# Products with block-diagonal adjacencies as 64 by 64 pieces in the four quarters of TensorE's array, with another order of steps

## The reference

```python
# layer 0: two hypergraph convolutions, G = D^-1 H B^-1 H^T from H = (adj != 0), with layer norm between
h = layer_norm(relu(G @ (x @ W1.T) + b1), gamma, beta)      # 512 -> 1024
y = G @ (h @ W2.T) + b2 + x                                  # 1024 -> 512
# layer 1: pairwise attention
A = exp(leaky(tanh((s_i + s_j) / 8) * 8)) * adj;  A = A / rowsum(A) * rowsum(adj);  y = A @ x @ w
# layer 2: three graph convolutions, relu after the first two
x = relu(adj @ (x @ W1) + b1); x = relu(adj @ (x @ W2) + b2); y = adj @ (x @ W3) + b3
# layer 3: attention of 8 heads over the 64 nodes, plus 0.33 * adj + 0.33 * exp(-adj), then an output projection
```

## Time and profile before

| | |
|---|---|
| median of 3 runs | 3037.49 us |
| lowest, highest | 3035.02, 3038.24 us |
| span of the profiled execution, first to last instruction | 3035.8 us |
| PE busy | 2912.6 us, 96% |
| PE weight loads busy | 2497.7 us, 82% |
| DVE busy | 2008.2 us, 66% |
| ACT, POOL busy | 922.4, 908.4 us, 30% each |
| one round of stage one | 76.50 us |
| one round of stage two | 106.0 to 106.1 us |

### The profile page before, as it was taken

The page is one execution under the profiler, slowest core; times in us unless marked ns, Lnnn a source line. Parts: engine busy times, 40 slices in busy tenths (PEclk is TensorE's granted clock), DMA queues, the critical chain, the costliest instruction groups (busy, mean ns, idle before and its releaser), DMA issues.

```text
span 3035.8 us, 50423 instructions
## 1 busy us (share of the span) xinstructions
PE 2912.6 (96%) x17944; PEld 2497.7 (82%) x17944; DVE 2008.2 (66%) x5274; ACT 922.4 (30%) x2525; POOL 908.4 (30%) x1619
## 2 busy tenths in 40 slices
PE   6999999999999999869999999999999999999998
PEld 4888888888888888658888888888888888888887
DVE  5888888888888888645455546545554654555465
ACT  2222222222222222133333324333332433333243
POOL 1222222222222222241342243134224313422431
PEclk9999999999999999979999999999999999999999
DMA  5000000000000000020010001001000100100000
GB/s 166 25 29 29 29 29 29 29 29 29 29 29 29 27 28 26 25 74 19 13 30 29 7 25 30 18 13 30 28 6 26 30 18 13 30 28 6 27 28 15
DMA packets 84785, 88.30 MB, mean 29 GB/s; under 512 B 46096, under 2 KB 46096, under 8 KB 84752
## 3 DMA queue, kind: packets, MB, share of 16 engines
q1 hardware_dynamic: 84752, 87.88, 9.5%
HBM read 54.28 MB, written 33.55 MB: 29 GB/s over the span
## 4 chain that ended last, share of the span: by engine, by line
PE 51%; DVE 3%; ACT 2%; DMA 1%; issue 0%; POOL 0%; DVEq 0%; POOLq 0%; SPq 0%
PE qsB L1070 30%; PE qsA L1070 16%; ACT E L941 2%; PE qsA L1136 2%; DVE E L1037 1%; PE qsA L1151 1%; PE qsA L1112 1%; PE qsA L1144 1%; PE qsB L1144 1%; DVE E L1024 1%; DMA X<-x 0%; DVE lo L970 0%; DMA QK<-in_L_Wqkv 0%; PE qsB L1086 0%; ACT hi L954 0%
## 5 line engine op out<-in xcount | busy, mean ns | idle before, releaser
L841 POOL TENSOR_SCALAR sm<-sm 128x1 f32<-128x1 f32 x128 | 28.5, 222 | 1064.9 <-DVE sm L987 1064.7
L982 DVE TENSOR_TENSOR T2l<-qsA,T2h 128x512 fp32r<-128x512 f32 x320 | 214.5, 683 | 198.0 <-ACT T2h L920 155.3
L219 POOL TENSOR_SCALAR sm<-sm 128x1 f32<-128x1 f32 x192 | 70.5, 367 | 835.8 <-DVE sm L430 666.8
L1070 PE MATMUL qsB<-hi,T2h 128*128 128x512 f32 x768 | 316.7, 412 | 1.4 <-DVE T2l L982 1.4
L1070 PE MATMUL qsB<-lo,T2h 128*128 128x512 f32 x768 | 304.1, 396 | 0.0
L1070 PE MATMUL qsB<-hi,T2l 128*128 128x512 f32 x768 | 303.9, 396 | 0.0
L941 ACT ACTIVATE E<-E,sm 128x128 f32<-128x128 f32 x512 | 198.2, 389 | 51.0 <-DVE sm L1028 51.0
L924 ACT ACTIVATE H<-H 128x512 f32<-128x512 f32 x128 | 81.0, 633 | 415.5 <-DVE H L1002 415.5
L541 PE MATMUL psA<-W2h,Th 128*128 128x512 f32 x512 | 205.1, 401 | 0.0
L541 PE MATMUL psA<-W2h,Tl 128*128 128x512 f32 x512 | 202.2, 395 | 0.0
L541 PE MATMUL psA<-W2l,Th 128*128 128x512 f32 x512 | 202.2, 395 | 0.0
(11 more groups left out here) (215 smaller groups left out, 8358.5 us busy)
## 6 DMA issues: line engine op xcount, KB each, us to landing
X<-in_x SPq DMA_DIRECT2D x64, 256.0 KB, 2.6
x<-R SPq DMA_DIRECT2D x64, 256.0 KB, 2.0
X<-x SPq DMA_DIRECT2D x64, 256.0 KB, 2.8
out<-Z SPq DMA_DIRECT2D x64, 256.0 KB, 2.9
A<-in_adj SPq DMA_DIRECT2D x256, 16.0 KB, 1.9
E<-in_L_W1T SPq DMA_DIRECT2D x4, 512.0 KB, 7.9
E<-in_L_W SPq DMA_DIRECT2D x4, 512.0 KB, 5.4
E<-in_L_Wqkv SPq DMA_DIRECT2D x2, 768.0 KB, 5.5
```

The costliest lines, as they stand in the source:

```text
L219: pool.tensor_scalar(col(c, VE), col(c, MV + 1), EPS, None, ALU.add).then_inc(ve, 1)
L982: return dve.tensor_tensor(lo, ps, hi.bitcast(F32), ALU.subtract)
L1070: mm = pe.matmul(out, lhsT, rhs, start=i == 0, stop=i == len(terms) - 1)
```

## The change

The 128 by 128 product becomes four products of 64 by 64 pieces: for each half of the features (q, which is also the half of the array's columns and of the output's rows) and each graph (g, the half of the array's rows), only the graph's own block is streamed, 64 columns. The zeros are left out. Each graph has its own bank: graph 0 writes psA, graph 1 psB, at 64 columns for each 128 features. The two banks of a chain are now one tensor `ps[c]`, and the evictions read both banks in one instruction.

```diff
-            def mix(out, rows, M):
-                for j in range(KD):
-                    f = slice(j * P, (j + 1) * P)
-                    mm = products(out[:, f], [(rows[:, f], M)])
+            def mix(c, rows, M, n):
+                for k in range(n):
+                    for q in (slice(0, C), slice(C, P)):
+                        for g, bank in ((slice(0, C), psA[c]), (slice(C, P), psB[c])):
+                            mm = pe.matmul(bank[q, k * C:(k + 1) * C], rows[g, k * P + q.start:k * P + q.stop], M[g, g],
+                                           start=True, stop=True)
                 return mm
+            def alone(sem, value):
+                pe.wait_ge(consts_ok, 4)
+                pe.wait_ge(sem, value)
             def tx(c, n, loaded):
-                pe.wait_ge(gt_sb, n[c])
+                alone(gt_sb, n[c])
                 pe.wait_ge(x_in[c], loaded)
                 pe.wait_ge(z2, n[c])
-                mix(psA[c][:, :], X[:, c, :], GT[:, c, :]).then_inc(tx_ps, 1)
+                pe.wait_ge(g1_sb, n[c])
+                mix(c, X[:, c, :], GT[:, c, :], KD).then_inc(tx_ps, 1)
             def t2(c, n):
-                pe.wait_ge(rc_ok, n[c])
+                alone(rc_ok, n[c])
                 pe.wait_ge(g2_ok, n[c])
-                mix(psA[c][:, :], R[:, c, 0:D], GT[:, c, :]).then_inc(t2_psA, 1)
-                mix(psB[c][:, :], R[:, c, D:DH], GT[:, c, :]).then_inc(t2_psB, 1)
+                mix(c, R[:, c, :], GT[:, c, :], KH).then_inc(t2_psA, 1)
...
-                products(psB[c][:, P:P + 1], [(Fp[:, c, :], ones[:, 0:1])])
-                mix(psA[c][:, :], R[:, c, D:DH], Fp[:, c, :]).then_inc(t3_ps, 1)
+                products(psB[c][:, 3 * P:3 * P + 1], [(Fp[:, c, :], ones[:, 0:1])])
+                mix(c, R[:, c, D:DH], Fp[:, c, :], KD).then_inc(t3_ps, 1)
...
             def txe(c, n):
                 act.wait_ge(tx_ps, n[c])
-                act.copy(Th[:, c, 0:D], psA[c][:, :]).then_inc(t1h, 1)
+                act.copy(by_graph(Th, c), halves(c)).then_inc(t1h, 1)
```

More of the change, by code:

```diff
@@ L90, in col, with halves, by_graph @@
             return sm[:, c, k:k + n]
-        psA = [ctx.enter_context(nc.psum_tensor(f"psA{c}", [P, D], F32)) for c in range(CH)]
-        psB = [ctx.enter_context(nc.psum_tensor(f"psB{c}", [P, D], F32)) for c in range(CH)]
+        ps = [ctx.enter_context(nc.psum_tensor(f"ps{c}", [P, 2, D], F32)) for c in range(CH)]
+        psA, psB = [ps[c][:, 0, :] for c in range(CH)], [ps[c][:, 1, :] for c in range(CH)]
+        def halves(c):
+            return ps[c][:, :, 0:KD * C].rearrange("p g (k j) -> p k g j", k=KD)
+        def by_graph(W, c, n=KD):
+            return W[:, c, 0:n * P].rearrange("p (k g j) -> p k g j", k=n, g=2)
         consts_ok, ident0 = sem("consts_ok"), sem("ident0")
@@ L288, in t2e @@
                 act.wait_ge(t2_psA, n[c])
-                act.copy(Th[:, c, 0:D], psA[c][:, :]).then_inc(t2hA, 1)
-                act.wait_ge(t2_psB, n[c])
-                act.copy(Th[:, c, D:DH], psB[c][:, :]).then_inc(t2hB, 1)
+                act.copy(by_graph(Th, c, KH)[:, :, 0, :], psA[c].rearrange("p (k j) -> p k j", k=KH)).then_inc(t2hA, 1)
+                act.copy(by_graph(Th, c, KH)[:, :, 1, :], psB[c].rearrange("p (k j) -> p k j", k=KH)).then_inc(t2hB, 1)
             def s8(c, n):
@@ L306, in t3e @@
                 act.wait_ge(t3_ps, n[c])
-                act.copy(Th[:, c, 0:D], psA[c][:, :]).then_inc(t3h, 1)
+                act.copy(by_graph(Th, c), halves(c)).then_inc(t3h, 1)
             def w(i):
@@ L395, in txe @@
                 dve.wait_ge(t1h, n[c])
-                dve.tensor_tensor(Tl[:, c, 0:D], psA[c][:, :], Th[:, c, 0:D].bitcast(F32), ALU.subtract).then_inc(t1_sb, 1)
+                dve.tensor_tensor(by_graph(Tl, c), halves(c), by_graph(Th, c).bitcast(F32), ALU.subtract).then_inc(t1_sb, 1)
             def relu(c, n, stored):
@@ L453, in t3e @@
             def t3e(c, n):
[L454 to L455 removed]
+                dve.wait_ge(t3h, n[c])
+                dve.reciprocal(col(c, RI), psB[c][:, 3 * P:3 * P + 1]).then_inc(ri_ok, 1)
                 dve.wait_ge(ri_ok, n[c])
                 dve.tensor_tensor(col(c, CI), col(c, RI), ATc[:, c, P:P + 1], ALU.mult)
[L458 to L459 removed]
+                dve.tensor_tensor(by_graph(Tl, c), halves(c), by_graph(Th, c).bitcast(F32), ALU.subtract).then_inc(t3_sb, 1)
             def z_second(c, n, after):
@@ L721, in col, with halves, by_graph @@
             return sm[:, c, k:k + n]
-        psA = [ctx.enter_context(nc.psum_tensor(f"qsA{c}", [P, D], F32)) for c in range(CH)]
-        psB = [ctx.enter_context(nc.psum_tensor(f"qsB{c}", [P, D], F32)) for c in range(CH)]
+        ps = [ctx.enter_context(nc.psum_tensor(f"qs{c}", [P, 2, D], F32)) for c in range(CH)]
+        psA, psB = [ps[c][:, 0, :] for c in range(CH)], [ps[c][:, 1, :] for c in range(CH)]
+        def halves(c):
+            return ps[c][:, :, 0:KD * C].rearrange("p g (k j) -> p k g j", k=KD)
+        def by_graph(W, c):
+            return W[:, :, c * P:(c + 1) * P].rearrange("p k (g j) -> p k g j", g=2)
         consts_ok, ident0, blocks0, bias_in, split_hi, split_lo = map(sem, (
@@ L919, in steps @@
                         act.wait_ge(t_ps[i], n[c])
-                        act.copy(T(Th, c), by_chunk(psA[c])).then_inc(th[i], 1)
+                        act.copy(by_graph(Th, c), halves(c)).then_inc(th[i], 1)
                     if step in ("g0", "g1"):
@@ L997, in steps @@
                         dve.wait_ge(th[i], n[c])
-                        rest(T(Tl, c), by_chunk(psA[c]), T(Th, c)).then_inc(t_sb[i], 1)
+                        rest(by_graph(Tl, c), halves(c), by_graph(Th, c)).then_inc(t_sb[i], 1)
                     if step in ("g0", "g1"):
@@ L1065, in _, with alone @@
             pe.wait_ge(consts_ok, 5)
+            def alone(sem, value):
+                pe.wait_ge(consts_ok, 5)
+                pe.wait_ge(sem, value)
             def products(out, terms):
@@ L1096, in steps @@
                         if i == 0:
-                            pe.wait_ge(at_sb, n[c])
+                            alone(at_sb, n[c])
                             pe.wait_ge(x_in[c], x_loaded[ahead])
                         else:
-                            pe.wait_ge(g_sb[i - 1], n[c])
+                            alone(g_sb[i - 1], n[c])
+                        rows = (H if i else X)[:, c, :]
                         for k in range(KD):
-                            f = slice(k * P, (k + 1) * P)
-                            mm = products(psA[c][:, f], [((H if i else X)[:, c, f], AT[:, c, :])])
+                            for q in (slice(0, C), slice(C, P)):
+                                for g, half in ((slice(0, C), psA[c]), (slice(C, P), psB[c])):
+                                    mm = pe.matmul(half[q, k * C:(k + 1) * C], rows[g, k * P + q.start:k * P + q.stop], AT[g, c, g],
+                                                   start=True, stop=True)
                         mm.then_inc(t_ps[i], 1)
```

10 lines of the change are left out of this document (6 added, 4 removed), and 24 rows, old and new, of the table ORDER.

## The result

The changed kernel takes 3065.3 us, the median of 4 runs (3062.38 to 3065.84). The kernel before, run beside it, takes 3037.2 us, also 4 runs. The ratio is 1.0094, with a 95% interval of 1.008 to 1.0108: slower by 0.9%. I had forecast 3012 us and a small gain. The time lies in the range that I gave, but on the wrong side of no change.

The account below looks back on a forecast made before the run. TensorE was taken to set the end: its work falls 5.45 and 3.8 us a round in stages one and two, added waits return 4.0 and 3.7, leaving 25 us saved over 16 rounds: 3012 us, range 2940 to 3090.

Parts of the forecast that it names:

- two at a time: Rival: the array's four quarters work only two at once, 0.90 us a run, 3085 us in all; chance 0.14.
- issue alone: Rival: issuing products at some 0.06 us each sets a run's time, 1.0 us, 3130 us in all; chance 0.08.
- feeding binds: Rival: handing products to TensorE limits a run to 0.64 us, 3033 us in all; chance 0.11.
- (a): Stage one: deg.0+ behind [tx.3 t2.1 t2.2] waits 1.6 us for inc.0+ from VectorE.
- (b): Stage one, after y2.2: deg.2+ waits 1.25 us for z1.2 and inc.2+, then y3.0 0.35 us for t3e.0.
- (c): Stage one: y3.1 after [t3.1 tx.0+] waits 0.8 us for z1.3 and t3e.1.
- (d): Stage one: tx.1+ and tx.2+ wait 0.2 and 0.15 us for z2; y3.3 waits 0.3, y2.3 0.1.
- (e): Stage two: g2.1 after [t2.1 t1.3 t2.2] waits 1.35 us, plus 0.1 for t2.2's relu.
- (f): Stage two, [t1.1 t2.0 t1.2 t0.3]: t1.2 waits 0.4 us for its relu, g2.0 1.1 for t2.0's eviction.
- (h): Stage two: av.2 waits 1.1 us for VectorE's copy of ta.2; g0.0+, behind z4.1 and av.3, waits 0.65.
- (i): Stage two: ta.2's wait for the softmax of s.2 falls from 1.97 to 0.45 us, with 0.4 before av.1.
- Nothing else is large: Both stages: beyond TensorE's work and the waits, evictions from two banks, added waits and DMAs taken to add about nothing.

Follow-up runs that it names:

- q_rot: The changed kernel with y1.2 and y2.0 moved from the end of stage one's TensorE loop to its head, same sequence; 3022.84 us, ratio 0.9957.
- w_neworder: Whole 128 by 128 products as in the kernel before, in both new orders; 3025.33 us, 0.9965 of the kernel before.
- part: Kernel before with quarters for t2 in stage one; stage two in new order, quarters for four steps only; 40 added instructions; 3020.3 us, ratio 0.9946.
- half: `q_rot` with stage two's evictions of t0, t1 and t2 covering half the columns in its rounds; 2995.85 us, 0.9866 of the kernel before.
- pad158: The changed kernel with 158 more instructions on TensorE's queue ahead of stage one's loop; 3043.2 us.
- q_oldorder: Quarter products with both stages' orders as in the kernel before; 3053.89 us, 1.0059 of the kernel before.

## Why the prediction was wrong

**What a run costs in quarters: right.** In `q_rot` the products of two t2 steps, four runs, stand as one group:

```profile
450.71 2.09 PE L577 MATMUL ps<-GT,R 64*64 64x64 f32 x128
```

Less some 0.24 us that the last takes to land, that is 1.85/4 = 0.46 us a run. All four quarters work at once, and no handover binds. The rivals "two at a time" (0.90) and "issue alone" (1.0) are out, and so is "feeding binds" (0.64). Two neighbouring runs of a chain each start 0.47 to 0.51 us apart (410.40 to 410.91 for t3.1 and tx.0+), so 0.45 was a little low.

**The evictions at no cost: right.** VectorE's rest out of both banks takes 685 ns in stage two and 678 to 684 in stage one, against 683 and 667 to 690 before (the earlier trace rows shows two of these).

**The waits: right in size.** Stage one, in `q_rot`: (a) 1.59 for 1.6, (b) 1.21 for 1.25 but nothing for the 0.35 before y3.0, (c) 0.84 for 0.8, (d) 0.31 twice for 0.2 and 0.15; TensorE idle for 75.50 - 71.05 = 4.45 of the 4.75 forecast. Stage two: (e) 1.01 for 1.35, (f) 0.34 and 0.71 for 0.4 and 1.1, (g) 0.50 for 0.5, (h) 0.86 and 1.24 for 1.1 and 0.65, (i) 0.52 and 0.32 for 0.45 and 0.4; idle (1396.20 - 1322.91)/13 = 5.6 of 6.0. `w_neworder` shows that the same order hardly waits when the products are whole, and `part` and `half` that the waits are for the evictions.

**The step that failed: "Nothing else is large".** I asked of each part what it adds to VectorE, to the banks and to the waits, and of the instructions only what it costs to hand them over. Their number nearly doubled in stage one's loop, and what that does to where they come from was no term of the sum. In stage one it costs, by `q_rot` and `pad158` against the changed kernel, 78.8 - 75.5 = 3.3 us a round. In the round shown, TensorE stands for 1.77, 0.35 and 0.70 us, less the 1.6 us of wait (a), which this covers: 1.2 us. Its work is longer by 73.06 - 71.05 = 2.0 us, since the products of t2 run at low clock (3.96 us from 388.46 to 392.42, the pause of 0.35 included, instead of the 1.85 above). At 14 jumps back 3.3 us are 46 us, more than the whole difference of the change (28 us).

**The sign would have been luck.** Without the fetching the changed kernel is `q_rot`, at 0.9957, where I had forecast 0.992. But its 13 rounds of each stage are not shorter than those before:

```profile
174.20:1155.30 981.10, 923.75 (x10349) 761.49 (x10349) 814.62 (x1977) 246.26 (x572) 294.47 (x468) 1.00 0.09 30
1468.70:2866.10 1397.40, 1323.45 (x12949) 1122.50 (x12948) 784.09 (x2288) 476.48 (x1456) 439.71 (x832) 1.00 0.08 23
```

They sum to 2378.5 us, for 2376.8. I had forecast 1.55 us less for the two rounds together; they are 0.1 more. All of `q_rot`'s gain lies outside these rounds, in a span that is 16.8 us shorter (3019.0 for 3035.8), and the start and end parts were no term of the sum of their own. Why the new orders shorten them was not looked into.

The 0.70 us before adjT.0+, which the profile puts down to the adjacency's load, are no wait of their own either: `pad158` has the changed kernel's loop, with the same step first behind the jump, and no such wait, and `w_neworder`, with this step first and whole products, has none either. A releaser is inferred, and here the fetch stands in the same place; I take the 0.70 us for part of it, without having shown it.

**A term that was mis-sized: TensorE's work in stage two.** I had 3.8 us less a round; measured (1355.78 - 1322.91)/13 = 2.5. With waits 3.6 longer (5.6 for 2.0) instead of 3.7, stage two loses 1.1 us instead of gaining 0.1. About half of the missing 1.3 is the order's own: with whole products it has 104.56 us of work instead of 104.04, where I had credited it with 0.15 less. In stage one the work fell by 75.75 - 71.05 = 4.7 instead of 5.45, which 16 runs at 0.02 to 0.05 more explain in good part. The rest was not taken apart.

**The new order itself.** I took both orders as given and found almost all of the gain handed back. `q_oldorder` shows that the handing back was the order's: old order, 73.8 us in stage one, of which TensorE idles 2.2; new order, 75.5 with 4.45 idle. There, single mixing steps between projections leave VectorE the time for its chains, and that is worth more than the shape changes saved by grouping them, which show as 0.6 us of work (71.64 for 71.05). In stage two the stretch without a jump says the same: 104.3 us in the old order, 107.2 in the new.

## What to carry to other kernels

Before an instruction is split into many inside a loop, count the loop body in instructions and look at the instruction queue of the page: here bodies of up to 1635 instructions were kept (22 to 25 packets in a whole run, about one for each 256 instructions of the program), one of 1617 was fetched in every round in one place and never in another, and one of 2019 always. Where one engine waits for chains on another, grouping its short steps costs more than changing shape for each: try the faster products in the old order before writing a new one, and each stage by itself. Whatever makes a busy engine's work shorter is worth what is saved less what is then waited, and a `half` of the suspected wait tells which it is.

## What the hardware showed that I had not expected

The same instructions in the same order take 3.3 us a round more or less by where the code lies. In stage two a fetch of ten packets a round (140 of `q_rot`'s 168, at 14 jumps back) cost next to nothing in the new order: the changed kernel's last stretch, without a jump back, takes 107.2 us, its rounds 107.4. In the old order nine packets go with a pause of 3.65 to 4.54 us. Why it differs was not tried.

The clock fell to 0.51 for 3.5 us behind a stretch in which TensorE had stood for 0.70 and 1.77 us with 0.7 us of work between, and to 0.55 for 3.5 us behind `q_oldorder`'s 4.54 us (1641.0 to 1644.5). The wait of 1.59 us before deg in `q_rot`, with full work up to it, left the round's clock at 1.00. A low clock in a window was the quickest sign that something was wrong that no wait names.
